# Cross attention on one core: the output of six batches normalised on GpSimd after a row swap over DMA, instead of through TensorE transposes

## What is computed

```python
Q = (query @ Wq.T + bq).reshape(B, Sq, N_HEADS, D_K).transpose(0, 2, 1, 3)
K = (key_value @ Wk.T + bk).reshape(B, Skv, N_HEADS, D_K).transpose(0, 2, 1, 3)
V = (key_value @ Wv.T + bv).reshape(B, Skv, N_HEADS, D_K).transpose(0, 2, 1, 3)
scores = jnp.einsum('bhqd,bhkd->bhqk', Q, K) / np.sqrt(D_K)
attn = jax.nn.softmax(scores, axis=-1)
context = jnp.einsum('bhqk,bhkd->bhqd', attn, V)
context = context.transpose(0, 2, 1, 3).reshape(B, Sq, D_MODEL)
x = context @ W_o.T + b_o + query
mu, var = mean(x), mean(square(x - mu))          # over the last axis
return (x - mu) / sqrt(var + 1e-5) * ln_gamma + ln_beta
```

## Time and profile before

| what | value |
|---|---|
| device time, median of 3 runs | 141.80 us (141.06 to 141.84) |
| the profiled execution | 141.58 us, its span 139.8 us |
| busy share PE, DVE, ACT, POOL | 93%, 69%, 64%, 59% |
| granted TensorE clock, mean | 0.996 of full speed |

### The profile page before, as it was taken

One profiled execution on the slowest core, in us unless ns is written; L12 is line 12 of the kernel. 1 busy time (PEld: TensorE's weight loads), 2 busy tenths in 40 slices (PEclk: granted clock), 3 DMA queues, 4 the chain that ended last, 5 costly groups with the idle time before them and its releaser, 6 DMA issues.

```text
span 139.8 us, 3936 instructions
## 1 busy us (share of the span) xinstructions
PE 130.3 (93%) x1477; PEld 114.1 (82%) x1477; DVE 96.5 (69%) x225; ACT 90.0 (64%) x187; POOL 82.0 (59%) x105
## 2 busy tenths in 40 slices
PE   4999999999989999989999999989999999999960
PEld 3899966789779988888989898979899878878720
DVE  5997799988657854876678856765687787521442
ACT  0887545288494929686766867665957758787620
POOL 8358899995542834105289967720589007498271
PEclk9999999999999999999999999999999999999998
DMA  4997685984479822671154036532270100011102
GB/s 128 324 364 257 242 259 187 288 282 118 108 183 333 235 67 75 214 224 17 58 186 150 7 103 196 202 134 72 93 273 0 44 0 5 8 36 33 38 0 66
DMA packets 16099, 19.59 MB, mean 140 GB/s; under 512 B 2624, under 2 KB 15488, under 8 KB 16080
## 3 DMA queue, kind: packets, MB, share of 16 engines
q1 hardware_dynamic: 14960, 17.42, 38.7%
q0 software_dynamic: 640, 1.64, 4.7%
q10 hardware_dynamic: 480, 0.28, 0.7%
HBM read 6.30 MB, written 0.92 MB: 52 GB/s over the span
## 4 chain that ended last, share of the span: by engine, by line
PE 73%; DVE 10%; SPq 6%; DMA 5%; issue 2%; ACTq 1%; POOLq 0%; ACT 0%; DVEq 0%
PE m_bank L882 17%; PE pv_bank L994 13%; PE mx_bank L943 12%; PE st_bank L976 12%; DVE mx L749 6%; PE m_bank L1026 4%; PE st_bank L882 3%; DMA k_stack<-k_hl 3%; PE mx_bank L1066 3%; SPq L266 3%; PE m_bank L1005 2%; PE mx_bank L976 2%; DMA q_stack<-shift 2%; SPq L358 2%; PE m_bank L903 2%
## 5 line engine op out<-in xcount | busy, mean ns | idle before, releaser
L749 DVE TENSOR_REDUCE mx<-mx_bank 112x1 f32<-112x375 f32 x128 | 63.7, 540 | 22.1 <-PE mx_bank L943 21.8
L632 ACT ACTIVATE pw<-st_bank 125x448 f32<-125x448 f32 x86 | 45.3, 546 | 18.4 <-PE st_bank L976 18.0
L943 PE MATMUL mx_bank<-k_stack,q_stack 128*112 128x376 f32 x128 | 43.7, 354 | 1.0 <-DMA k_stack<-k_hl 0.5
L976 PE MATMUL st_bank<-q_stack,k_stack 128*125 128x224 f32 x172 | 34.8, 284 | 0.6 <-DMA q_stack<-shift 0.4
L976 PEld LDWEIGHTS st_bank<-q_stack,k_stack 128*125 128x125 f32 x172 | 28.6, 186 | 4.1 <-issue 1.5
L943 PEld LDWEIGHTS mx_bank<-k_stack,q_stack 128*112 128x112 f32 x128 | 22.1, 176 | 4.5 <-DVE mx L749 1.8
L430 POOL TENSOR_TENSOR k_hl<-k_full,k_hl 128x376 fp32r<-128x376 f32 x10 | 10.0, 1002 | 20.9 <-ACT k_hl L549 20.9
L994 PE MATMUL pv_bank<-pw,v_sb 125*17 125x112 f32 x744 | 21.5, 260 | 0.0
L994 PEld LDWEIGHTS pv_bank<-pw,v_sb 125*17 125x17 f32 x744 | 16.7, 97 | 3.1 <-issue 1.9
L882 PE MATMUL m_bank<-w_hl,c_hl 128*125 128x256 f32 x126 | 18.2, 282 | 0.0
L882 PEld LDWEIGHTS m_bank<-w_hl,c_hl 128*125 128x125 f32 x126 | 17.3, 186 | 0.0
(11 more groups left out here) (113 smaller groups left out, 177.7 us busy)
## 6 DMA issues: line engine op xcount, KB each, us to landing
k_stack<-k_hl SPq DMA_DIRECT2D x48, 188.0 KB, 2.7
c_raw<-ctxT SPq DMA_DIRECT2D x7, 375.0 KB, 4.3
q_stack<-q_hl SPq DMA_DIRECT2D x9, 112.0 KB, 2.2
x_space<-x_nat SPq DMA_DIRECT2D x4, 224.0 KB, 3.1
out<-yo SPq DMA_DIRECT2D x8, 112.0 KB, 2.0
pw<-wT SPq DMA_DIRECT2D x2, 256.0 KB, 4.3
q_stack<-q_hl POOLq DMA_DIRECT2D x3, 168.0 KB, 2.8
q_stack<-q_hl SPq DMA_DIRECT2D x3, 168.0 KB, 2.8
```

The costliest lines, as they stand in the source:

```text
L632: nc.scalar.activation(p_tile[0:KC, n % PR, :, :], st_of(n)[0:KC, 0:4 * Q].rearrange("p (j q) -> p j q", j=4), ACT.Exp, scale=float(DK) ** ...
L749: nc.vector.tensor_reduce(mx[b % 2][:, h % 2, q_pair(h // 2):q_pair(h // 2) + 1], mx_bank[n % MR][0:Q, 0:KV], axis=AX_X, op=ALU.max, negat ...
L943: nc.tensor.matmul(mx_bank[n % MR][0:Q, 0:KVP], q_stack[k][:, side, q_pair(h // 2), b - Q_STACKS[k][0], :], k_stack[b % 3][:, h // 2, :], ...
L976: last = nc.tensor.matmul(st_of(n)[0:KC, k * 2 * Q:(k + 1) * 2 * Q], k_stack[i % 3][:, 2 * g + k, c * KC:(c + 1) * KC], q_stack[qk][:, :, ...
```

## The change

For batches 0 to 5 the six transposes of the output and the DVE work between them are gone. V's tile now has 32 weight columns for each head, V's columns and ones in turn (`VW = 2 * DK`), so that each group of 32 output partitions holds a row of output and a row of denominator in turn, in all 16 pairs. Of the two head groups that share a half of the output, the first gives its even rows and the second its odd rows:

- ACT at u = 1 copies all of `pv_bank` to `o_raw` (`take_raw`), and at u = 2 (`take_o`) one half of its columns to `o_normT` and the other half to `den`. For the second copy it waits for `o_scaled`, the count of batches that POOL has multiplied, since there is one `den` only.
- SP moves odd rows of `o_raw` to even rows of `den`, and even rows to odd rows of `o_normT` (`swap_rows`, two DMAs of 64 x 2 x 112).
- DVE takes the reciprocal of `den` (128 x 224) a batch later at u = 1 (`invert`).
- POOL multiplies and adds V's bias (`scale_output`), two operations of 128 x 224, behind `scale_rows` of the batch before in its queue.
- `out_project` moves from three batches later at u = 0 to two batches later at u = 5, and `layer_norm` to u = 7; at the end they are at (6,8) for batch 4 and (7,5) for batch 5.

Further edits: `stack_q(3)` (Q's last stack, 6 DMAs) is issued by SP ahead of `stack_shift(4)` in iteration 3, behind which it stood; the maxima's transpose moves from u = 6 to 7 in batches 2 to 5 and stands ahead of the products with V; POOL does `bias_into_x` ahead of `context_lo`, and clears V's third tile at the start (128 x 1536); DVE's memset before PE's first matmuls is 128 x 512 instead of 128 x 816; ACT copies ones into V's second tile at the start. The weights of the output projection and V's bias are put in the new row order on the host.

```diff
-VW = DK + 1
+VW = 2 * DK
-U_MT = (8, 7, 6, 6, 6, 6, 5)
+U_MT = (8, 7, 7, 7, 7, 7, 4)
+OUT_AT = {i: U_OUT for i in range(2, B - 2)} | {B - 2: 8, B - 1: 5}
+NORM_AT = {i: U_LN for i in range(2, B - 2)} | {B - 2: 8, B - 1: 5}
...
+            def swap_rows(b):
+
+                sp.wait_ge(o_raw_ready, b + 1)
+                raw = o_raw[b % 2][:, :].rearrange("p (e s q) -> p e s q", e=EC, s=2)
+                sp.dma_start(den[0:PART - 1:2, :, :], raw[1:PART:2, :, 0, :]).then_inc(swap_in[b % 2], 16)
+                sp.dma_start(o_normT[b % 2][1:PART:2, :, :], raw[0:PART - 1:2, :, 1, :]).then_inc(swap_in[b % 2], 16)
...
+            def scale_output(b):
+
+                pool.wait_ge(rden_ready, b + 1)
+                nc.gpsimd.tensor_tensor(o_normT[b % 2][:, :, :], o_normT[b % 2][:, :, :], den[:, :, :],
+                                        op=ALU.mult).then_inc(o_scaled, 1)
+                pool.wait_ge(o_scaled, b + 1)
+                pool.wait_ge(bv_in, 16)
+                nc.gpsimd.tensor_tensor(o_normT[b % 2][:, :, :], o_normT[b % 2][:, :, :],
+                                        bv[:, :].unsqueeze(2).to_broadcast([PART, EC, Q]),
+                                        op=ALU.add).then_inc(o_normT_ready, 1)
...
+                if i >= 2:
+                    scale_output(i - 2)
+                if 2 <= i < 2 + B // ROWS:
+                    bias_into_x(i - 2)
...
             for b in range(B - V_AHEAD - 3, B - 1):
                 inverse_deviation(b)
                 scale_rows(b)
+                if b + 1 < B - 2:
+                    scale_output(b + 1)
...
+            def take_raw(b):
 
                 act.wait_ge(pv_done, NG * (b + 1))
                 if b >= 2:
-                    m, n = m_job("OT", b - 2)
-                    act.wait_ge(m_full[m], n + 1)
-                nc.scalar.copy(o_raw[b % 2][:, :], pv_bank[:, 0:NG * Q]).then_inc(o_raw_ready, 1)
+                    act.wait_ge(swap_in[b % 2], 32 * (b // 2))
+                nc.scalar.copy(o_raw[b % 2][:, :], pv_bank[:, 0:NG * Q])
+
+            def take_o(b):
+
+                src = pv_bank[:, 0:NG * Q].rearrange("p (e s q) -> p e s q", e=EC, s=2)
+                if b >= 2:
+                    wait_full(act, "OUT", b - 2)
+                nc.scalar.copy(o_normT[b % 2][:, :, :], src[:, :, 0, :])
+                if b >= 1:
+                    act.wait_ge(o_scaled, b)
+                nc.scalar.copy(den[:, :, :], src[:, :, 1, :]).then_inc(o_raw_ready, 1)
...
+            def invert(b):
+                dve.wait_ge(swap_in[b % 2], 32 * (b // 2 + 1))
+                nc.vector.reciprocal(den[:, :, :], den[:, :, :]).then_inc(rden_ready, 1)
...
+                    if u == U_INVERT and 2 <= i < B - 1:
+                        invert(i - 2)
+                    if u == 6 and i == B - 2:
+                        invert(B - 3)
```

199 lines of the change are left out of this document (96 added, 103 removed).

## The result

| | median (runs) | profiled execution | its span | first exponential at |
|---|---|---|---|---|
| before | 141.49 us (141.06 to 141.84, 4) | 141.6 us | 139.8 us | 24.18 us |
| after | 152.72 us (151.58 to 153.03, 4) | 153.0 us | 151.2 us | 24.86 us |

What follows compares the result with a forecast made beforehand. TensorE, busy for 93% of the span, was taken to bound the kernel. From 141.6 us, savings of 5.1 and added costs of 4.4, 1.2, 1.2, 1.1, 0.4, 0.4 and 0.9 gave 146.1 us, range 141.5 to 149.0.

Steps and rivals of the forecast that it cites:

- the third rival: Only batch 3's wait binds, those of batches 4, 5 and 7 vanish: 141.7 us, no change; chance 0.10.
- The end: TensorE waits 1.1 us for batch 5's projection at (7,5), behind DVE's normalisation and POOL's rows of batch 4.
- the late reciprocal of batch 4: In batch 6 DVE's reciprocal at u = 1 pushes `o_raw` and the products behind it by about 0.4 us.
- The clock: Rival: the clock falls to 1.2 GHz in batch 3's long wait, costing 2 us more, 148.1; chance 0.13.
- Batch 3: ACT's copy into `den` waits for POOL's product behind memsets and row operations; TensorE waits 4.4 us before (3,5).
- Batches 4 and 5: The same wait for POOL's product as in batch 3, without memsets: TensorE waits 1.2 us in each.
- What goes: Savings on TensorE: 3.8 us of transposes, 0.5 for the wait ahead of them, 0.8 for K; together 5.1.
- The wait for K: TensorE's wait for a K stack at 91.93 goes as Q's DMAs are issued before the shift; 0.8 us saved.
- Wide weights at nothing: Weight loads of 32 columns instead of 17 in the products with V stay hidden and cost nothing.
- The 0.9 of batches 6 and 7: Where ACT's exponentials pace, 0.9 us of the removed projection and transposes doesn't come back; between 0 and 1.5.
- 0.2 once: DVE's reciprocal of 224 elements, 1.3 us, takes `layer_norm`'s place at u = 1 and adds 0.2 us in batch 2.
- The start: A shorter first memset gains 0.3 us, work on V's ones loses it; 0.2 us set for both ends.

Runs made afterwards that it cites:

- x3_dve_end: Kernel after with only DVE's order in batch 6 changed: reciprocal of batch 5 behind the layer norm of batch 4; 148.28 us, 1.049 of before.
- x2_pool_end: Kernel after with only the end of POOL's queue changed: product and bias of batch 5 ahead of batch 4's row operations; 147.8 us, 1.042 of before.
- x5_two_den: Kernel after with two tiles of denominators in turn instead of one, POOL's queue unchanged; 147.46 us, 1.042 of before.
- x4_fill_end: Kernel after with eight unused fp32 matmuls on TensorE ahead of the wait for batch 5's output projection; 151.0 us, 1.070 of before.
- x1_pool_loop: Kernel after with POOL's product and bias ahead of the row operations in its loop, and Q's clearing behind batch 1's product; 147.66 us, 1.045 of before.
- x6_clear_late: Kernel after with only the clearing of Q's last stack moved, behind the product of batch 1 on POOL; 149.62 us, 1.060 of before.
- x8_before_q_first: Kernel before with only the six DMAs of Q's last stack moved ahead of batch 4's shift on SP; 141.33 us, 1.0005 of before.
- x7_before_w32: Kernel before with V's ones widened from 1 to 16 columns a head, so weight loads have 32 columns; 142.68 us, 1.011 of before.
- y3_fixed_light: Kernel after with two `den` tiles, POOL's products first, Q's last stack behind the shift, and half-column exponentials in batches 2 to 7; 141.46 us, 1.001.
- y2_before_light: Kernel before with exponentials of batches 2 to 7 over the first half of their columns only; 140.59 us, 0.997 of before.
- w2_whole: Kernel after with two `den` tiles, POOL's products first, batches 0-2's projections in unit 0 three batches later, their layer norms in unit 3; 140.98 us, 0.998.
- z2_out0_halves: Kernel after with two `den` tiles, POOL's products first, batches 0-3's projections in unit 0, halved reciprocals, Q's last stack issued in batch 4; 154.21 us, 1.089.
- y4_halves: Kernel after with two `den` tiles, POOL's products first, Q's last stack behind the shift, and reciprocals halved over units 1 and 2; 141.8 us, 1.0035.

## Why the prediction was wrong

It said 146.1, up to 149.0; it is 152.7. (The range takes the third rival at 141.5, its own sum gives 141.7; that changes nothing.) Direction and first mechanism were right. Against the profiled execution of 153.0 us, 6.9 are missing: 5.0 in batch 7, 1.3 in batch 3, 0.5 ahead of the first exponential, 0.1 in the rest.

**The step that failed** is "The end", the wait of 1.1 for batch 7. The wait measured 4.15 us, and with the clock's fall behind it, some 2 us, the batch became 6.1 longer. The chain that I followed ("from the projection's start to the end of `mv` it is 2.2 us") holds for a DVE that is free. The change puts the reciprocal of batch 5 ahead of that layer norm, and I never asked what it waits for: a swap that SP issues at 122.46 and 123.17, since ACT's copy waits for POOL's product of batch 4, and this for DVE, and that lands only at 127.0. With the two in the other order the wait was 1.14 us (x3_dve_end), with the product first on POOL none (x2_pool_end). With two tiles it was 1.41 (x5_two_den), but most of that is the shorter transfer and not the earlier issue. I had named the late reciprocal of batch 4 and given it 0.4, without following it to the next reciprocal.

**The clock** was set apart as a rival with 0.13 and 2 us once. It fell in both long waits. The size was right: 1.7 in batch 3, by its rows, and 2.4 in batch 7, by the profile of x4_fill_end (1.7 by its median). What spoke against it in my text, that the clock held through an idle stretch behind the last matmul, was weak, as the fall came later there as well. In batch 3 it began 1.3 us after TensorE was back at work.

**Batch 3.** Right as a mechanism and nearly in size: ACT's copy at 79.25 (said 79.5), TensorE's wait 3.35 us (said 4.4, since I took its arrival 0.9 too early; 0.53 of that is a wait for maxima behind the reciprocal, which I did not have in this batch). x1_pool_loop and x6_clear_late show the cause: the memsets.

**Batches 4 and 5**, 1.2 us each, were right by accident. ACT waited for POOL as described (its copy into `den` waits 1.75 us in batch 4), but that cost TensorE only 0.26 and 0.24 us. What made up the rest is a wait of 0.92 us at each batch's start that I did not have: the projection's 0.86 us had stood there beside K's copies on ACT for nothing, and in unit 5 it is paid. I had subtracted the projection's 0.86 from TensorE's arrival and not asked what it had covered.

**What goes.** 0.63 us a batch shows in batch 1 (0.6). The wait ahead of the transposes in batch 2 is gone. The wait for K, 0.8, was one execution's (x8_before_q_first). Wide weights at nothing: right within 0.2 us in the batches of one execution; the 1.5 us by which the median of x7_before_w32 lies above before is open. The 0.9 of batches 6 and 7 was near in size by luck: batch 6 lost a projection and transposes of 0.86 + 0.63 and became 0.3 shorter, so 1.2 did not come back, but ACT's exponentials do not pace it (y3_fixed_light). TensorE, busy there for 10.47 of 10.47 us before, now waits for the last maxima, which stand on DVE behind the reciprocal of batch 4. The change also asks for them at u = 4 and not at u = 5; no run parts the two. TensorE's and DVE's timelines of the kernel after, and TensorE's of the kernel before:

```profile
122.77 0.26 PE L1007 MATMUL m_bank<-ident,mx 112*16 112x112 f32 x1 [0.89 <-DVE mx L788]
```

```profile
121.23 1.39 DVE L788 TENSOR_REDUCE mx<-mx_bank 112x1 f32<-112x375 f32 x3
```

```profile
119.36 0.26 PE L958 MATMUL m_bank<-ident,mx 112*16 112x112 f32 x1
```

The reciprocal takes 1.54 us, not 1.3, and two blocks of maxima wait 0.53 us behind it, in batches 2 and 3, where I had 0.2 once.

**The start**, 0.68 us later in the profile where I had 0.2 for both ends, can't be told from scatter: kernels whose start is that of the kernel before (x8_before_q_first, y2_before_light) show it at 24.8 and 24.9.

**What stays open.** In w2_whole the long waits are mended but for that in batch 6, and 0.2 us of the 3.8 remain, less than its interval can tell from nothing. Batches 1 and 2 are 0.5 and 0.3 shorter, batches 5 and 6 together some 0.6 longer than the kernel before's. The projection of batch 3 has moved from batch 6 into batch 5. Its trace also shows waits that the kernel before doesn't have: 0.48 and 0.37 us behind DVE in batches 2 and 3, three of 0.34 (0.07 to 0.08 idle) for an exponential in batches 2 to 4, 0.64 for the shift ahead of batch 6, and 0.88 idle for the last maxima in batch 6, in all 3.4 us, about as much as the transposes cost. No run takes these away one by one, and the 1.5 us of x7_before_w32 may have a part in it; so where the saving went is read from rows and not shown.

## What to carry to other kernels

When an operation with a wait is put into an in-order queue, follow two things: what it waits for, back through every engine until something is surely early (a single buffer can close a ring there), and what stands behind it in the queue. Ask of work that is moved away what wait it had covered; moved, it costs its length, even if it is no longer than before. A wait of some microseconds on TensorE should be priced with a fall of the clock behind it, half of the busy time that it spends at the lower level, as a likely cost and not a sure one.

## What the runs showed of the hardware

- The clock fell late and came back later. In the kernel after it went to 1.2 GHz behind waits of 3.35 and 4.15 us; it stayed there for 3.4 us in batch 3 and 6.8 in batch 7. Behind the wait in batch 3 it fell 1.3 us after TensorE was at work again, and in four other kernels with a wait of that size there from 0.1 us before to 1.4 after (x3_dve_end, x5_two_den, x4_fill_end, x2_pool_end). It stayed at 2.4 GHz in the profiled executions with waits of 1.6 and 2.2 us (x1_pool_loop, x6_clear_late, batch 4), and when matmuls with an unused result filled the wait (x4_fill_end).
- The length of the wait alone does not tell. In z2_out0_halves the clock fell at 130.35, 1.4 us after TensorE was at work again behind only 1.59 us of idle time. And one of the four executions of x2_pool_end and of x5_two_den shows hardly a fall (mean granted clock 0.999 and 0.997, 146.03 and 145.82 us, 1.4 us or more below the others), with the same instructions as the rest.
- DVE's reciprocal on fp32 costs by the element: 840 ns for 128 x 112 and 1545 for 128 x 224, 6.3 ns for each further one. The groups of y4_halves and of the kernel after:

```profile
L830 DVE RECIPROCAL den<-den 128x112 f32<-128x112 f32 x12 | 10.0, 840 | 0.8 <-DMA o_normT<-o_raw 0.8
```

```profile
L826 DVE RECIPROCAL den<-den 128x224 f32<-128x224 f32 x6 | 9.3, 1545 | 3.4 <-DMA o_normT<-o_raw 3.4
```

- The Trainium skill ("VectorE: DVE Perf Modes", section "First, the fixed hardware budget") says that a reciprocal is an iterative divide with a repeat count of 8. That it is dear for each element agrees with the rows: 6.3 ns, where the maxima of 375 elements take 538 ns on the same engine, 1.4 ns an element with all fixed cost in it. The count of 8 no run here shows. From 4 and 16 elements I had read 5.1 ns.
